# A hybrid attention, mixture-of-experts and RWKV kernel: ScalarE's share of the token shifts, three subtractions moved or removed, 21 more weights in two halves, and all steps placed anew

## The reference

```python
x = x + attention(layernorm(x), W_Q, W_K, W_V)        # causal, one head of 128
x = x + moe(layernorm(x))                             # 32 experts, top 4, capacity, and a shared expert
x = x + rwkv(layernorm(x))
x = x + moe(layernorm(x))                             # the same weights again
```

```python
h = layer_norm(x, ln1_w, ln1_b);  hh = time_shift(h)          # the token before
xk = h * att_tmk + hh * (1 - att_tmk)                         # likewise xv, xr
k, v, sr = xk @ Wk.T, xv @ Wv.T, sigmoid(xr @ Wr.T)
# scan over the tokens, with carries aa, bb and the running maximum pp:
qq = max(pp, u + kt);  e1 = exp(pp - qq);  e2 = exp(u + kt - qq)
y = (e1 * aa + e2 * vt) / (e1 * bb + e2)
qq2 = max(pp + w, kt); aa, bb = exp(pp + w - qq2) * aa + exp(kt - qq2) * vt, ...
x = x + (sr * y) @ Wo.T
h = layer_norm(x, ln2_w, ln2_b);  hh = time_shift(h)          # and again a token shift
kk = square(relu((h * ffn_tmk + hh * (1 - ffn_tmk)) @ Wkey.T));  kv = kk @ Wval.T
x = x + sigmoid((h * ffn_tmr + hh * (1 - ffn_tmr)) @ Wrec.T) * kv
```

## Time and profile before

| | us |
|---|---|
| median of 3 runs | 793.85 |
| lowest and highest | 793.61, 794.05 |
| span of the profiled execution | 791.7 |
| outside that span (median less span) | 2.1 |

### The profile page before, as it was taken

The page is one execution under the profiler, slowest core; times in us unless marked ns, Lnnn a source line. Parts: engine busy times, 40 slices in busy tenths (PEclk is TensorE's granted clock), DMA queues, the critical chain, the costliest instruction groups (busy, mean ns, idle before and its releaser), DMA issues.

```text
span 791.7 us, 12780 instructions
## 1 busy us (share of the span) xinstructions
PE 785.1 (99%) x3817; PEld 596.4 (75%) x3817; DVE 645.9 (82%) x1539; ACT 567.9 (72%) x1055; POOL 625.3 (79%) x491
## 2 busy tenths in 40 slices
PE   8999999999999999999999999999999999999998
PEld 5777778676776777768778777887778767788786
DVE  6875577997997989998988869988689889767686
ACT  5677787868768778689765867668685775677553
POOL 6687779849767797769987888998797877876985
PEclk9999999999999999999999999999999999999999
DMA  9353334243144342462425444253444424425552
GB/s 326 95 123 82 87 92 113 66 102 92 42 113 113 73 105 54 110 133 58 120 60 134 104 93 107 65 143 79 110 113 95 90 68 110 111 59 115 124 127 74
DMA packets 49332, 80.73 MB, mean 102 GB/s; under 512 B 3280, under 2 KB 14544, under 8 KB 48880
## 3 DMA queue, kind: packets, MB, share of 16 engines
q1 hardware_dynamic: 48976, 79.72, 42.1%
q10 hardware_dynamic: 288, 0.20, 0.1%
HBM read 75.19 MB, written 4.72 MB: 101 GB/s over the span
## 4 chain that ended last, share of the span: by engine, by line
PE 51%; POOL 2%; issue 2%; DVE 1%; ACT 0%; DVEq 0%; POOLq 0%; ACTq 0%
PE pa L1039 5%; PE pb L1039 4%; PE py L1067 4%; PE pa L1043 4%; PE pb L1043 4%; PE pa L1040 4%; PE pb L1040 4%; PE pu L1326 4%; PE py L1072 3%; PE py L1074 3%; PE py L1073 3%; POOL m_h L587 1%; PE pq L1283 1%; PE pu L1310 1%; PE pv L1334 1%
## 5 line engine op out<-in xcount | busy, mean ns | idle before, releaser
L587 POOL TENSOR_TENSOR m_h<-m_v,m_wb 128x512 f32<-128x512 f32 x254 | 364.3, 1444 | 98.7 <-DVE m_v L1468 42.9
L732 ACT ACTIVATE m_th<-pa 128x512 f32<-128x512 f32 x220 | 130.6, 594 | 102.0 <-PE pa L1043 97.7
L1468 DVE TENSOR_TENSOR m_v<-m_th,pb 128x512 f32<-128x512 f32 x205 | 138.6, 679 | 23.9 <-ACT m_th L732 15.5
L1039 PE MATMUL pa<-m_xh,w1h 128*128 128x512 f32 x272 | 137.2, 504 | 0.3 <-DVE m_v L1471 0.2
L416 DVE TENSOR_TENSOR m_hl<-m_h,m_hh 128x512 fp32r<-128x512 f32 x120 | 111.4, 929 | 24.8 <-ACT m_hh L921 24.1
L921 ACT ACTIVATE m_hh<-m_h 128x512 fp32r<-128x512 f32 x184 | 115.2, 626 | 13.8 <-POOL m_h L587 13.1
L1039 PE MATMUL pb<-m_xh,w3h 128*128 128x512 f32 x272 | 115.4, 424 | 0.0
L1043 PE MATMUL pa<-m_xl,w1h 128*128 128x512 f32 x272 | 107.3, 394 | 0.3 <-POOL m_xl L608 0.3
L1043 PE MATMUL pb<-m_xl,w3h 128*128 128x512 f32 x272 | 107.1, 394 | 0.0
L1040 PE MATMUL pa<-m_xh,w1l 128*128 128x512 f32 x272 | 106.6, 392 | 0.0
L1040 PE MATMUL pb<-m_xh,w3l 128*128 128x512 f32 x272 | 106.5, 391 | 0.0
(11 more groups left out here) (318 smaller groups left out, 1653.8 us busy)
## 6 DMA issues: line engine op xcount, KB each, us to landing
m_wb<-w_scratch SPq DMA_DIRECT2D x126, 512.0 KB, 6.5
x_sb<-in_x SPq DMA_DIRECT2D x8, 256.0 KB, 7.2
m_wb<-in_w SPq DMA_DIRECT2D x2, 1024.0 KB, 6.8
x_out<-x_sb SPq DMA_DIRECT2D x7, 256.0 KB, 6.6
u_scratch<-t_u SPq DMA_DIRECT2D x6, 256.0 KB, 2.6
t_u<-u_scratch SPq DMA_DIRECT2D x6, 256.0 KB, 2.7
f_kk<-in_w SPq DMA_DIRECT2D x1, 1024.0 KB, 9.7
w_scratch<-r_wT SPq DMA_DIRECT2D x16, 64.0 KB, 1.5
```

The lines of the kernel that those rows point to most:

```text
L587: pool.tensor_tensor(hidden(g, p), gated(g, p), m_wb[:, p % (GRING * GP), :], ALU.mult).then_inc(sig["m_h"], 1)
L732: ins = act.activation(m_th[:, p % 2, :], pa[p % 2][:, :], ACT.Silu)
L1039: pe.matmul(ps[:, :], high[:, p, :], xh, start=True, stop=False)
L1468: dve.tensor_tensor(gated(g, p), m_th[:, r, :], pb[r][:, :], ALU.mult).then_inc(sig["m_v"], 1)
```

## The change

It has four parts.

1. `NATIVE` shrinks from 88 to 67 units: 21 more are split. `LOW_ON_POOL`, `LOW_LATE` and `TANH` change with it. POOL makes 63 low halves of hidden units for 64 before, DVE 142 for 120, and 50 units take Tanh for 52.
2. `m_xl` is made by DVE, which reads the high-precision value from PSUM. PE waits for it before it overwrites that bank with the logits.
3. The token shifts: ACT multiplies the shifted tile by `1 - factor` (`rest`), and DVE adds `h * factor` to that. POOL's differences `t_d` (but for the last sequence) and `f_d` go.
4. The exponents: one difference per pair is left, `a = pp + w - k` and `b = u + k - pp`. ACT takes Relu of it and of its negative, then Exp of minus both. The maximum on DVE and both differences on POOL go.

All slot tables are new, those of the opening too. SP's issues are not changed.

```diff
 NATIVE = (
-    (3, 9),
+    (3,),
+    (),
...
+        rest = sb("rest", [P, 11])
...
@@ POOL
-                if slot == (20, 19, 37, 23, 18, 19, 15, 26, 42, 25, 36, 21, 35, 21, 40, 34)[q]:
-                    pool.wait_ge(sig["r_xT"], q + 1)
-                    pool.wait_ge(sig["m_xh"], q + 1)
-                    pool.tensor_tensor(m_xl[:, q % 2, :], r_xT[:, :], m_xh[:, q % 2, :].bitcast(F32),
-                                       ALU.subtract).then_inc(sig["m_xl"], 1)
...
-                if slot == (26, 24, 24, 23, 25, 30, 32, 25)[m]:
-                    pool.wait_ge(sig["t_pp"], m + 1)
-                    pool.tensor_tensor(t_ea[:, 1, :], t_k[:, :], t_pp[:, 1:1 + S], ALU.subtract).then_inc(sig["t_a1"], 1)
-                if slot == (29, 29, 28, 29, 43, 32, 33, 30)[m]:
-                    pool.wait_ge(sig["t_qq"], m + 1)
-                    pool.tensor_tensor(t_eb[:, 0, :], t_pp[:, 0:S], maxima(m), ALU.subtract).then_inc(sig["t_b0"], 1)
...
@@ ACT
+                if slot == (31, 32, 32, 30, 45, 36, 32, 33)[m]:
                     act.wait_ge(sig["t_a0"], m + 1)
+                    act.activation(t_ea[:, 1, :], t_ea[:, 0, :], ACT.Relu).then_inc(sig["t_ra"], 1)
+                if slot == (33, 34, 33, 32, 50, 37, 39, 35)[m]:
+                    act.wait_ge(sig["t_ra"], 2 * m + 1)
+                    act.activation(t_ea[:, 0, :], t_ea[:, 0, :], ACT.Relu, scale=-1.0).then_inc(sig["t_ra"], 1)
...
+            def kept_part(m, dst, c, read, times):
...
+                    act.activation(dst[:, :], t_h[:, 0:S], ACT.Identity, scale=rest[:, c:c + 1]).then_inc(sig["t_g"], 1)
+
+            def kept_blend(m, dst, c):
...
+                act.activation(dst[:, :], f_h[:, 0:S], ACT.Identity, scale=rest[:, c:c + 1]).then_inc(sig["f_keep"], 1)
...
@@ PE, opening
             def first_step(slot):
-                if slot == (23,)[0]:
+                if slot == (22,)[0]:
                     up_gate(0, 0)
                     up_linear(0, 0)
-                if slot == (28,)[0]:
+                if slot == (22,)[0]:
                     up_gate(0, 1)
...
@@ PE, router logits
                         pe.wait_ge(sig["m_xh"], q + 1)
+                        pe.wait_ge(sig["m_xl"], q + 1)
...
@@ DVE, att_step: row_stats, then row_moments, then normalise
-                if slot == (0, 7, 8, 1, 1, 11, 9, 13)[n]:
+                if slot == (5, 5, 8, 0, 5, 15, 11, 14)[n]:
...
-                if slot == (0, 7, 9, 1, 2, 11, 17, 13)[n]:
+                if slot == (5, 10, 8, 0, 11, 18, 15, 14)[n]:
...
-                if slot == (2, 10, 14, 8, 16, 16, 21, 19)[n]:
+                if slot == (6, 11, 11, 4, 17, 18, 22, 17)[n]:
...
@@ DVE, weights_step
-                if slot == (2,)[0]:
+                if slot == (6,)[0]:
                     high_part(w1h[:, 0:PAIRS, :], w_stage[:, 0:PAIRS, :], "in_w1")
-                if slot == (12,)[0]:
+                if slot == (6,)[0]:
                     high_part(w3h[:, 0:PAIRS, :], w_stage[:, PAIRS:2 * PAIRS, :], "in_w3")
...
@@ DVE, pro_step
+                if slot == (22, 23, 23, 17, 21, 19, 18, 24, 16, 25, 20, 20, 21, 25, 28, 13)[q]:
+                    dve.wait_ge(sig["r_xT"], q + 1)
+                    dve.wait_ge(sig["m_xh"], q + 1)
+                    dve.tensor_tensor(m_xl[:, q % 2, :], router_bank(cmix)[:, :], m_xh[:, q % 2, :].bitcast(F32),
+                                      ALU.subtract).then_inc(sig["m_xl"], 1)
...
@@ DVE, time_begin: the maximum goes
-                if slot == (28, 29, 30, 26, 37, 35, 34, 29)[m]:
-                    dve.scalar_tensor_tensor(out=maxima(m), in0=t_k[:, :], scalar=vec[:, FIRST:FIRST + 1],
-                                             in1=t_pp[:, 0:S], op0=ALU.add, op1=ALU.max).then_inc(sig["t_qq"], 1)
...
@@ DVE, mix
-                    dve.scalar_tensor_tensor(out=dst[:, :], in0=t_d[:, :], scalar=vec[:, c:c + 1], in1=t_h[:, 0:S],
+                    dve.scalar_tensor_tensor(out=dst[:, :], in0=t_h[:, 1:1 + S], scalar=vec[:, c:c + 1], in1=dst[:, :],
```

More of the change, by code:

```diff
@@ L47 @@
 NATIVE = (
[15 rows of a table removed]
+    (3,),
+    (),
+    (2, 3, 5, 6, 9, 10, 11, 12, 13),
+    (1, 2, 3, 4, 5, 9, 10, 11, 12, 13, 14, 15),
+    (3, 5, 6, 7, 9, 11, 16),
+    (1, 2, 7, 10, 11, 12, 13),
+    (1, 5, 7, 9, 15),
+    (1, 9),
+    (1, 3, 7, 9, 11),
+    (1, 3, 5, 7, 9),
+    (3, 5, 7, 11, 15),
+    (1, 7, 9),
+    (3, 7, 11),
+    (),
+    (11,),
     (13, 16),
@@ L275, in hybrid_kernel @@
         w2_stage = f_kk[:, :, :].rearrange("p a (b c) -> p (a b) c", c=P)
-        f_hn, f_h, f_d, f_xk, f_xr = a_xn, a_xT, a_g, a_p, a_pT
+        f_hn, f_h, f_xk, f_xr = a_xn, a_xT, a_p, a_pT
         f_g = a_p[:, :]
@@ L854, in time_begin @@
                     act.wait_ge(sig["t_rps"], m + 1)
                     act.activation(t_r[:, :], pq[:, :], ACT.Tanh, scale=0.5).then_inc(sig["t_r"], 1)
-                if slot == (34, 36, 35, 35, 37, 36, 39, 31)[m]:
+                if slot == (31, 32, 32, 30, 45, 36, 32, 33)[m]:
                     act.wait_ge(sig["t_a0"], m + 1)
-                    act.wait_ge(sig["t_a1"], m + 1)
-                    act.activation(wide(t_ea[:, :, :]), wide(t_ea[:, :, :]), ACT.Exp).then_inc(sig["t_expa"], 1)
@@ new lines, in time_begin @@
+                if slot == (32, 34, 38, 33, 38, 34, 33, 31)[m]:
+                    act.wait_ge(sig["t_b1"], m + 1)
+                    act.activation(t_eb[:, 0, :], t_eb[:, 1, :], ACT.Relu).then_inc(sig["t_rb"], 1)
+                if slot == (37, 35, 39, 39, 43, 35, 34, 34)[m]:
+                    act.wait_ge(sig["t_rb"], 2 * m + 1)
+                    act.activation(t_eb[:, 1, :], t_eb[:, 1, :], ACT.Relu, scale=-1.0).then_inc(sig["t_rb"], 1)
+                if slot == (33, 34, 35, 35, 51, 38, 40, 35)[m]:
+                    act.wait_ge(sig["t_ra"], 2 * m + 2)
+                    act.activation(wide(t_ea[:, :, :]), wide(t_ea[:, :, :]), ACT.Exp, scale=-1.0).then_inc(sig["t_expa"], 1)
@@ L865, in channel_step @@
+                if slot == (38, 36, 40, 40, 51, 37, 40, 38)[m]:
+                    act.wait_ge(sig["t_rb"], 2 * m + 2)
+                    act.activation(wide(t_eb[:, :, :]), wide(t_eb[:, :, :]), ACT.Exp, scale=-1.0).then_inc(sig["t_expb"], 1)
             def channel_step(m, slot):
-                if slot == (29, 37, 25, 36, 28, 34, 24, 36)[m]:
+                if slot == (31, 36, 29, 37, 30, 36, 26, 37)[m]:
                     act.wait_ge(sig["f_xk"], 2 * m + 1)
                     act.activation(f_xh[:, :], f_xk[:, :], ACT.Copy).then_inc(sig["f_xh"], 1)
-                if slot == (21, 25, 22, 24, 23, 28, 17, 26)[m]:
+                if slot == (23, 27, 21, 28, 22, 28, 13, 24)[m]:
@@ L1565, in pro_step @@
             def pro_step(q, slot, cmix):
-                if slot == (16,)[0] and q == 0:
+                if slot == (12,)[0] and q == 0:
                     dve.wait_ge(sig["a_add"], 2)
@@ L1787, in first_step @@
             def first_step(slot):
-                if slot == (27,)[0]:
+                if slot == (31,)[0]:
                     open_gate(0, 0)
```

388 lines of the change are left out of this document (202 added, 186 removed), and 13 rows, old and new, of the table NATIVE.

## The result

The changed kernel takes 805.23 us (median; 804.63 to 807.11), the kernel before 793.92 us in runs beside it. The ratio is 1.0149, with an interval from 1.0134 to 1.0163: 11.3 us slower. The forecast was 795.0, and the range ended at 799.5. The profiled execution has a span of 803.0 us.

The account below looks back on a forecast made before the run. PE, busy for 99% of the span, was taken as the bound. Terms -3.4 - 0.4 + 0.4 + 1.0 + 4.1 = +1.7 us on 791.7 gave 793.4, 795.5 as runs' median, stated as 795.0; range 791.0 to 799.5.

Parts of the forecast that it names:

- The wait in the opening: Opening: DVE stands still for sequence 1's load until 10.5, so a_xn starts 4.1 us later and PE's first unit at 27.5.
- new stalls up to the third unit: Opening, PE's less lucky order up to the third unit: 0.8 us, between 0 and 1.5.
- the opening's term: PE's late start carried through to the end: 4.1 - 0.8 + 0.8 = +4.1 us, between 2.5 and 5.5.
- No engine but PE is over 84%: Whole kernel: DVE comes to 84% of the span and ACT to 78%, so work moved there costs nothing on average.
- full stretches: Loop stretches where DVE is nearly full: +0.5 us for g 7, +0.5 for all others, +1.0 between -1 and +6.
- The forecast's own sign: Wrong if PE's distance from its first unit to the end doesn't fall by 2 to 3 us.
- the rivals: Late start made up, 791.9 us, chance 0.2; DVE's queue bounds PE, 798.6, 0.25; opening costs more, 797, 0.1.
- DVE's queue as PE's bound: Rival: in g 7 and at the waits for m_xl, PE waits for DVE, 798.6 us; chance 0.25.
- g 7: Loop stretch with DVE busy 41.22 of 45.80 us; four low halves and one m_xl more there cost +0.5 us.
- The splits: 21 native units split, each saving 0.16 us of PE: -3.4 us.
- m_xl: Made on DVE: the opening's stall goes, -0.4 us; PE's waits before 15 later logits cost +0.4 in all.
- that relief: By the shared-port rule, POOL's removed work relieves DVE; full stretches would cost nothing and the sum be 1 us lower.

Follow-up runs that it names:

- e3: The changed kernel with seven more filler matmuls on PE in the opening, before it transposes a_xn of sequence 0: ratio 1.0107 to the kernel before.
- e5: The kernel before with routing weights for g 1 to 15 read from those of g 0, without waiting for the router: ratio 0.9996.
- e13: The kernel before with the first group of routing weights of each iteration but the first loaded in two steps: ratio 0.9994.
- e9: The changed kernel with sequence 1's statistics at slot 8, routing loads not waiting for the router, and the old split tables from g 1 on: ratio 1.0022.
- e7: The kernel before with only the changed tables NATIVE, LOW_ON_POOL, LOW_LATE and TANH, 21 more split units: ratio 1.0211.
- e1: The changed kernel with DVE's statistics of sequence 1 at slot 8 instead of 5, behind attention 0's maxima: ratio 1.0095 to the kernel before.
- e12: The changed kernel with sequence 1's statistics at slot 8, loads in two steps, and routing weights' transposition and copy earlier in six iterations: ratio 1.0035.
- e11: The kernel before with the routing weights' transposition on PE and copy on ACT moved to the changed kernel's slots where later: ratio 1.0097.
- e6: The changed kernel with sequence 1's statistics at slot 8 and the router's last steps at the earlier of both kernels' slots where order allows: ratio 1.0271.
- e4: The changed kernel with routing weights for g 1 to 15 read from those of g 0, without waiting for the router: ratio 1.0065.
- e10: The changed kernel with sequence 1's statistics at slot 8 and each iteration's first routing-weight loads, but the first iteration's, in two steps: ratio 1.0000.

## Why the prediction was wrong

**The wait in the opening** was found, placed and priced: a_xn at 11.21 for 11.35, and 27.57 for 27.5 at the first unit once the clock is held (e3). The 0.8 us of new stalls up to the third unit didn't come: g 0 takes 50.61 us for 51.33. **The size of the opening's term** was off by the clock: +4.1 took it as given that PE's products cost what they had cost in the kernel before, whose granted clock was 1.0 there. A PE that idles as long as the forecast itself said has to be asked for its clock too. That is 1.7 us in the profiled execution, and more in those whose mean clock was 0.996.

**The step that failed** is "No engine but PE is over 84%, so on average these parts cost nothing", with the look at full stretches that follows it. I looked for stalls where an engine is full. The forecast's own sign for this was a distance from PE's first unit to the end that doesn't fall by 2 to 3 us: it grew by 6.3. The 6.7 to 7.5 us came from a chain that is hardly ever busy: counts, r_w, its transposition, its copy, a write to DRAM of 1.6 us, a load of 6.9 us, m_h. I had compared the slots of m_xl and the logits and not those of the tail behind them, although PE's transposition moved later in 11 of 16 iterations. It falls under none of the rivals. DVE's queue as PE's bound was named for g 7 and the logits, and neither is where the time went. POOL's 12.3 us of such waits in the kernel before, no measurable part of which reached PE (e5 0.9996, e13 0.9994), would have been the warning: the lead was used up already.

**The splits** were priced at -3.4 us. They saved 1.7 (e9), and that only with POOL relieved and the slots moved; with neither they cost 16.7 (e7). **m_xl** behaved as forecast: the stall of the earlier trace rows is gone, an instruction takes 689 to 691 ns for the 679 assumed, and PE's list has one wait for it, of 0.2 us. **g 7** took 45.65 us, 0.35 above the 45.3 of PE's work, where +0.5 was assumed. With both mishaps repaired the ratio is 1.0000 where the forecast without its opening term would have said 791.4, 0.9969.

**Busy times.** POOL's 567 for 561 and ACT's 608 for 619 are near; 56 table loads were right, and a scaling takes 719 ns for the assumed 0.7. DVE's 645 for 666 is the large miss. The low halves grew by 11.4 us and not by 20.5, since their mean fell from 929 to 866 ns. That is 9 of the 21 us. Most of the rest is spread over other operations on tiles in SBUF: the mixes of channel mixing (a_p from 1391 to 922 ns), f_xl (896 to 717), the residual x_sb behind them (887 to 709). The low halves rose to 945 in e7, where POOL keeps its 78%. The forecast had priced that relief at 1 us of PE and at nothing of DVE. The rule that it weighed (the Trainium skill, *SBUF — State Buffer*, "SBUF: two separate sides") agrees with the trace in the main: most operations with two SBUF inputs got shorter with POOL's share, and the gate's product, which reads PSUM, stayed at 679 ns. A few went the other way (t_eb times t_bb from 829 to 1059 ns), so POOL's share alone doesn't set the mean of each.

## What to carry to other kernels

When a table of slots is new, follow the longest chain with a DMA in it first, however idle its engines are, and write down its lead over the consumer in both kernels; a late lead shows up on the bound engine under another name. Where the lead is short, make the first piece of the transfer smaller rather than its producer earlier, as an in-order engine turns "earlier" into a wait. And where a forecast lets the tensor engine idle, price what comes behind at the lower clock as well.

## What the runs showed of the hardware

- In the opening of after PE had been busy for 1.85 of 4.00 us, and then the granted clock was 0.54 for 3.7 us. With 2.54 busy us of the same 4.00 (e3) or 3.31 (e1) it stayed at 1.00. In the middle of the loop one wait was enough: 2.55 us in e12, 1.8 in e11, each with a clock of 0.57 for 4.0 us behind it. In e12 that cost 1.6 us on top of the wait. e6's longest wait, 2.3 us, left it at 1.00.
- At the very start, PE's first products ran at half pace for up to 3 us longer in some profiles. The view shows a granted clock of 1.00 there, but the packed trace has no record of the clock before its first one, which gives the higher level. That one comes at 4.7 us in the kernel before, 4.6 in e4, 7.2 in e10, 7.4 in e1 and 7.5 in after, and the pace changes right there. So the 1.00 ahead of it is no measurement, and the pace fits the lower level. The same four transpositions follow for e4 and then for e10, whose programs for PE are the same up to there. What decides when the clock rises is open, and a first unit can be some 1 us late without any cause in the code.

```profile
5.27 0.60 PE L1016 MATMUL pu<-ident,x_sb 128*128 128x128 f32 x4
```

```profile
5.86 1.06 PE L1017 MATMUL pu<-ident,x_sb 128*128 128x128 f32 x4
```

- Landing hangs on size more than a fixed cost would have it: 512 KB in 6.8 us, 256 KB in 4.1 (the first step of e10). By the Trainium skill's fit (*SBUF — State Buffer*, "The DMA setup-cost knee": 2 us plus the bytes at 436 GB/s) it would be 3.2 and 2.6 us, an estimate. The measurement decides; these are transfers issued in pairs, half the partitions each.
